# A one-core two-layer attention and mixture kernel: the same steps issued in another order, from a new time table

## What is computed

```python
# cut from the reference
x = x + rotary_attention(conditioned_attention(x, mask, cond))      # 16 heads, causal rotary; inner one 16 heads of 8, rms norm, modulation
x = x + mixture_0(quaternion_filter(x, cond))                       # 8 experts of 128->512->128, the best 2 by a softmax over them
x = x + level_attention(mixture_1(x, cond))                         # 8 experts of 128->256->256->128; decay and level weights, layer norm
x = x + quantised_ffn(conditioned_attention_1(x, mask, cond))       # 128->512, 3-tap conv along the sequence, silu, ->128
```

## Time and profile before

| | us |
|---|---|
| median of 3 runs | 630.21 |
| lowest, highest | 629.35, 632.31 |
| the profiled execution, its own time | 623.68 |
| its span | 621.9 |
| busy in the span: PE, weight loads, VectorE, ScalarE, GpSimd | 473.9, 375.1, 303.5, 246.2, 171.4 |
| mean granted TensorE clock | 0.884 of 2.4 GHz |

### The profile page before, as it was taken

One profiled execution on the slowest core, in us unless ns is written; L12 is line 12 of the kernel. 1 busy time (PEld: TensorE's weight loads), 2 busy tenths in 40 slices (PEclk: granted clock), 3 DMA queues, 4 the chain that ended last, 5 costly groups with the idle time before them and its releaser, 6 DMA issues.

```text
span 621.9 us, 11762 instructions
## 1 busy us (share of the span) xinstructions
PE 473.9 (76%) x4233; PEld 375.1 (60%) x4233; DVE 303.5 (49%) x771; ACT 246.2 (40%) x683; POOL 171.4 (28%) x210
## 2 busy tenths in 40 slices
PE   4897989768989946587776978669998734778875
PEld 4685877557869924466665866544665624566432
DVE  3779655643334427511122247774554003776653
ACT  3545644314575541123332463232554422343311
POOL 5054343172220233550004003455100022232200
PEclk9999989975999977769998998876999985897888
DMA  7977540010444530137786663101263710000000
GB/s 246 325 203 148 160 135 2 2 43 18 132 130 124 154 90 22 47 94 201 185 214 198 171 185 93 27 9 42 61 172 90 182 50 18 2 3 0 1 9 9
DMA packets 50631, 62.13 MB, mean 100 GB/s; under 512 B 6704, under 2 KB 39664, under 8 KB 50320
## 3 DMA queue, kind: packets, MB, share of 16 engines
q1 hardware_dynamic: 48048, 56.88, 33.1%
q0 software_dynamic: 2048, 4.20, 2.3%
q10 hardware_dynamic: 480, 0.32, 0.2%
HBM read 52.86 MB, written 16.94 MB: 112 GB/s over the span
## 4 chain that ended last, share of the span: by engine, by line
PE 55%; DVE 18%; issue 10%; ACT 10%; POOL 3%; another core or an unknown queue 2%; DMA 2%; ACTq 0%; POOLq 0%; DVEq 0%
PE PS L852 6%; PE PS L842 6%; PE PS L826 4%; PE PS L1407 4%; PE PS L1439 4%; PE PS L1834 3%; PE PS L1224 2%; PE PS L1238 2%; PE PS L1421 2%; DVE arena L1735 2%; PE PS L838 2%; PE PS L1213 2%; ACT rot_sm L1494 2%; ACT hid L920 2%
## 5 line engine op out<-in xcount | busy, mean ns | idle before, releaser
L766 POOL DMA_INDIRECT picked<-slots_y,place_u x32 | 31.1, 971 | 109.4 <-DMA slots_y<-slot_y 100.9
L852 PE MATMUL PS<-expert_w,hid 128*128 128x128 f32 x360 | 54.0, 287 | 7.6 <-ACT hid L920 2.7
L852 PEld LDWEIGHTS PS<-expert_w,hid 128*128 128x128 f32 x360 | 46.4, 196 | 14.4 <-issue 10.0
L1072 DVE TENSOR_SCALAR hid<-PS,expert_w 128x128 f32<-128x128 f32 x60 | 18.3, 347 | 75.3 <-PE PS L842 42.2
L842 PE MATMUL PS<-hid,expert_w 128*128 128x128 f32 x240 | 35.7, 296 | 12.5 <-ACT hid L920 9.9
L920 ACT ACTIVATE hid<-PS,expert_w 128x128 f32<-128x128 f32 x120 | 37.4, 366 | 16.7 <-PE PS L826 10.6
L842 PEld LDWEIGHTS PS<-hid,expert_w 128*128 128x128 f32 x240 | 31.3, 204 | 17.0 <-issue 15.8
L826 PE MATMUL PS<-slot_xT,expert_w 128*128 128x128 f32 x240 | 40.0, 293 | 1.9 <-ACT slot_xT L910 1.9
L1439 PE MATMUL PS<-rot_W,rot_yT 128*128 128x128 f32 x256 | 34.3, 298 | 3.7 <-ACT rot_yT L1509 3.7
L1439 PEld LDWEIGHTS PS<-rot_W,rot_yT 128*128 128x128 f32 x256 | 32.8, 211 | 6.9 <-ACT rot_yT L1509 5.7
L826 PEld LDWEIGHTS PS<-slot_xT,expert_w 128*128 128x128 f32 x240 | 33.6, 202 | 4.8 <-ACT slot_xT L910 2.7
(11 more groups left out here) (277 smaller groups left out, 1058.1 us busy)
## 6 DMA issues: line engine op xcount, KB each, us to landing
expert_w<-packed SPq DMA_DIRECT2D x60, 514.0 KB
slot_x<-slots_x SPq DMA_DIRECT2D x60, 64.0 KB
slots_y<-slot_y SPq DMA_DIRECT2D x60, 64.0 KB
...
```

The lines of the kernel that those rows point to most:

```text
L766: nc.gpsimd.indirect_dma_start(picked[:, j, n, :], None, ys[half], bass.IndirectOffsetOnAxis(place_u[job % 2][:, j, n:n + 1], 0)).then_inc ...
L852: mm = nc.tensor.matmul(full(bank_of(MO_, i), 2 * P, 3 * P), hid[:, i % 2, c, :], W[i % WB][:, lo + E * (c - first):lo + E * (c - first) + ...
```

## The change

`TIMES` gets new numbers, nearly all of them. No step is added, removed or changed, and nothing outside the dictionary is touched. Comparing the two sorted orders gives the number of places at which another step stands than before: PE 403 of 526, ScalarE 353 of 457, VectorE 191 of 266, GpSimd 78 of 139, SyncE 64 of 188.

The places that the prediction speaks of:

- `f_taps_of_all` 0 to 3 on PE: before, all four ahead of `m_count` 0; after, all behind it, spread up to the middle of job 0's slots.
- `r_scores` 4 on PE: before, behind `m_biases` 0 and two places ahead of `m_transpose_slots` 0; after, right behind `m_count` 0. The projections of tile 4 come ahead of `m_count` 0.
- `r_times_x` and `r_output` of tiles 6 and 7: before, behind `m_slots_out` 14 (places 201 to 209 of PE, where `m_slots_out` 14 is 200); after, at places 167 to 184, ahead of it (place 208). `r_scores` 6 and 7 move from 197 and 199 to 150 and 170.
- `m_choose` 2 on VectorE: after, right behind `m_choose` 1 and ahead of `m_places` 1. The eight `m_scatter` of jobs 1 and 2 are contiguous on GpSimd, without another step between.
- In job 1, five times `m_hidden_a` of a slot stands ahead of the next slot's `m_transpose_slots` instead of behind it.
- `m_gates` 0 moves from place 331 to 309 of PE, `l_output` 0 from 348 (behind `m_slots_out` 44, which was 344) to 337 (ahead of it, now 349).
- GpSimd after job 2: before `l_inverse_deviation` 0, gathers 8, 9, `c1_spread_keys` 0, `c1_spread_values` 0, gathers 10, 11; after `l_inverse_deviation` 0, `c1_spread_values` 0, `c1_spread_keys` 0, gathers 8 to 11.
- VectorE there, before: combine 8, norm 1, conditioned softmax 0, combine 9, weights of scores 3, `c1_turn` 0, two norm steps, combines 10 and 11, a norm step, `m_squares` 1. After: level weights 2, conditioned softmax 0, norm 1, `c1_turn` 0, combines 8 and 9, weights of scores 2, level weights 3, a norm step, combines 10 and 11, `m_squares` 1.
- PE ahead of `m_transpose_slots` 45: before, eleven steps of `c1_`, `f_` and `m_biases` 3 from `c1_scores` 1 on; after, six of these stand ahead and five behind it.
- At the end, `f_bias` and `f_hidden` of tiles 4 and 5 come ahead of tile 7's `c1_transpose_x` and `c1_scores`.

The diff, cut to the entries of these steps:

```diff
--- before.py
+++ after.py
@@ -116,200 +116,203 @@
...
-    "m_gather": (210.3, 212.5, 214.8, 217, 303, 305.3, 307.5, 309.7, 351.7, 353.9, 358.5, 360.7, 460.4, 462.7, 464.9, 467.2),
-    "m_scatter": (113.9, 116.2, 118.4, 120.6, 233.4, 235.6, 237.8, 240, 245.8, 248.1, 250.3, 252.5, 377.9, 380.1, 382.3, 384.5),
-    "c1_spread_keys": (356.2, 372.2, 387.9, 401.7, 498.3, 501.8, 518.8, 523),
-    "l_inverse_deviation": (350.6, 363, 366.1, 371.2, 491.2, 494.5, 509.6, 513.7),
-    "f_taps_of_all": (86.8, 89.9, 97.9, 106.4),
-    "r_scores": (38.9, 43.9, 70.6, 79, 126, 156.7, 197.5, 202.1),
-    "r_times_x": (55.2, 75.1, 85.8, 92.4, 141.2, 167.7, 210.4, 226.9),
-    "r_output": (67, 82.3, 93.4, 101.4, 144.5, 171, 214.5, 231.1),
-    "m_gates": (335, 475.1),
-    "m_transpose_slots": (129.8, 132.7, 139.1, 140.2, 150.8, 153.5, 154.5, 164.1, 166.6, 168.6, 178.8, 179.8, 185, 188.9, 192.6, 248.4, 249.2, 253.8,
-        254.4, 256.9, 262.7, 265.5, 268.3, 271.9, 274.4, 277.5, 281.1, 284, 286.8, 290.6, 293.4, 296.2, 298.4, 301.1, 303.8, 306.5, 309.3, 313.8,
-        317.2, 324.6, 325.9, 330.6, 333.2, 334, 336.5, 392.9, 395, 397.8, 401.4, 408.1, 409.9, 416.9, 423.8, 430.3, 432.5, 438.1, 440.9, 442.2,
-        445.9, 451.1),
-    "m_choose": (108.3, 227, 239.4, 371.1),
-    "m_combine": (215.6, 217.9, 220.1, 222.5, 308.9, 310.6, 314.1, 317.9, 357, 361.1, 366, 366.7, 465.8, 468, 470.3, 472.5),
-    "c1_turn": (362.2, 383.7, 398.2, 411.2, 503.6, 509.8, 524.6, 532.6),
-    "f_hidden": (384.6, 401.5, 419.6, 427.3, 522.7, 532.7, 544.2, 549.3),
...
+    "m_gather": (225.46, 227.7, 229.94, 232.18, 318.23, 320.47, 322.71, 324.95, 368.2, 370.44, 372.68, 374.92, 476.68, 478.92, 481.16, 483.4),
+    "m_scatter": (120.14, 122.36, 124.58, 127.85, 248.68, 250.88, 253.08, 255.28, 257.48, 259.7, 261.92, 264.14, 392.64, 394.84, 397.04, 399.24),
+    "c1_spread_keys": (366.64, 403.75, 408.26, 442.07, 515.3, 519.99, 538.08, 550.22),
+    "l_inverse_deviation": (355.47, 377.16, 385.21, 401.44, 508.15, 511.48, 528.42, 532.28),
+    "f_taps_of_all": (120.13, 134.76, 161.99, 168.23),
+    "r_scores": (43.83, 50.39, 74.36, 83.1, 117.71, 144.49, 166.38, 183.89),
+    "r_times_x": (71.04, 79.78, 90.46, 94.45, 141.04, 163.07, 180.57, 194.58),
+    "r_output": (76.2, 86.9, 97.85, 106.3, 146.79, 169.09, 186.64, 197.97),
+    "m_gates": (335.04, 491.45),
+    "m_transpose_slots": (136.52, 137.74, 141.97, 151.84, 161.85, 163.99, 175.01, 179.95, 190.66, 192.87, 202.56, 205.43, 207.36, 210.1, 212.6,
+        265.2, 265.47, 270.72, 270.86, 274.05, 279.71, 282.15, 284.19, 288.47, 290.51, 293.37, 297.65, 299.69, 302.55, 306.83, 308.87, 311.73,
+        314.01, 316.91, 319.82, 322.73, 326.45, 329.74, 332.46, 336.7, 343.25, 345.26, 346.53, 350.03, 354.56, 407.56, 410.85, 413.77, 417.59,
+        421.63, 425.47, 428.94, 432.43, 436.74, 444.91, 446.51, 452.99, 457.17, 460.24, 466.81),
+    "m_choose": (113.74, 240.76, 243.67, 385.55),
+    "m_combine": (230.74, 232.98, 235.22, 237.46, 323.5, 326.44, 329.12, 331.81, 375.58, 376.28, 380.87, 381.58, 481.96, 484.2, 486.44, 488.68),
+    "c1_turn": (373.23, 415.55, 417.87, 448.76, 522.84, 528.31, 546.77, 556.33),
+    "f_hidden": (401.91, 432.56, 439.97, 462.61, 537.53, 542.63, 567.72, 575.42),
...
```

More of the change, by code:

```diff
@@ L118 @@
 TIMES = {
[L119 to L131, removed]
@@ new lines @@
+    "l_inverse_deviation": (355.47, 377.16, 385.21, 401.44, 508.15, 511.48, 528.42, 532.28),
[5 rows of a table added]
+    "p_modulations": (11.87,),
+    "c0_scores": (12.4, 14.69, 38.3, 42.86, 65.29, 91.38, 115.47, 143.34),
+    "p_turn_modulations": (17.52,),
+    "r_turn_weights": (16.6, 18.8),
+    "r_fold_weights": (20.79, 29.53, 41.95, 45.67),
[3 rows of a table added]
+    "p_turn_rotation": (31.37,),
[3 rows of a table added]
+    "p_rotations_pe": (36.3,),
+    "r_project_3": (35.28, 41.06, 60.49, 66.25, 112.68, 135.63, 153.27, 178.57),
+    "p_rotated_router": (41.03,),
@@ new lines @@
+    "p_copy_modulations": (18.63,),
+    "r_copy_turned": (17.99, 19.97),
+    "r_copy_folded": (22.76, 30.63, 43.23, 48.84),
[4 rows of a table added]
+    "p_copy_rotation": (31.67,),
+    "r_copy_passed_2": (36.07, 40.33, 64.13, 69.57, 105.6, 134.28, 161.69, 177.6),
+    "p_copy_rotations": (36.96,),
+    "r_copy_passed_3": (37.52, 42.61, 65.35, 70.18, 114.11, 136.71, 162.31, 179.81),
+    "p_copy_router": (41.25,),
+    "r_take_scores": (45.86, 57.05, 76.39, 86.24, 119.74, 146.52, 168.42, 185.92),
+    "r_exponentials": (51.47, 64.75, 82.96, 91.38, 133.24, 153.65, 173.55, 191.51),
@@ new lines @@
+    "f_copy_yqT": (408.63, 445.69, 453.37, 469.52, 546.63, 556.68, 578.83, 582.53),
+    "p_router": (9.28,),
+    "p_gated_condition": (11.08,),
+    "p_spread_condition": (8,),
+    "p_casts": (9.85,),
+    "p_mask_bias": (9.03,),
+    "p_norms": (11.77,),
+    "p_gains": (12.72,),
+    "c0_softmax_in": (14.73, 17.27, 39.44, 46.82, 71.65, 94.35, 120.03, 144.48),
+    "c0_turn": (19.32, 21.62, 43.73, 51.25, 76.3, 97.1, 123.75, 149.58),
+    "p_rotations": (25.29,),
+    "f_magnitudes": (23.92,),
[5 rows of a table added]
@@ L313 @@
+    "f_quantise_x": (393.62, 426.73, 431, 457.62, 532.81, 536.56, 559.8, 565.89),
+    "f_gate": (405.34, 436, 443.43, 466.06, 540.98, 546.09, 573.77, 578.88),
+    "f_quantise_y": (406.03, 436.68, 446.69, 466.74, 541.67, 549.46, 574.46, 579.56),
+    "f_finish": (412.16, 451.08, 456.42, 470.8, 549.09, 558.65, 581.63, 583.8),
 }
```

198 lines of the change are left out of this document (82 added, 116 removed), and 111 rows, old and new, of the table TIMES.

## The result

| | before | changed |
|---|---|---|
| median of 20 runs each, us | 629.39 | 630.50 |
| lowest, highest | 615.04, 640.60 | 625.91, 638.26 |
| profiled execution, its span | 623.68, 621.9 | 633.15, 631.4 |
| mean granted clock | 0.884 | 0.869 |

The medians of all 20 are only 0.2% apart; the ratio of the runs within 1.5% of the fastest of their kernel (5 of the 20 before, 17 of the 20 changed) is 1.016 (95% interval 1.0112 to 1.0208). Single executions of one kernel scatter by some 2% around their median here, so the comparison was made twice more with both kernels beside each other: 1.0137 (1.0067 to 1.0207) and 1.0223 (1.016 to 1.0285). The kernel before against itself gave 0.996 (0.9907 to 1.0013) and 1.0018 (0.9969 to 1.0067). The forecast was 615 and "faster"; it was wrong in sign, and the loss rests on the three ratios together.

The account below looks back on a forecast made before the run. PE was taken to bound the slots, and the gather, combine, choose, scatter chain the waits between jobs. The terms -1 -3 +5 -1.5 -1 -14 +1 -1 gave -15.5: 608.2 us profiled, 615 on the median, range 600 to 629.

Parts of the forecast that it names:

- +5: Job 0's slots (145 to 223): rotary tails and taps come in, projections leave; 5 us longer, from 0 to +12.
- 223 to 267: Wait after job 0: tails leave, the routing and scatter chain stays; -1.5 us, from -4 to +2.
- The main term, -14: Wait after slot 44 (377 to 436): shorter chain to job 3's first transpose, 2.9 + 6 + 1 + 4; from -16 to -7.
- The "6" between gather and squares: Wait after slot 44: gathers together and most DVE work after them save 6 of up to 7.8 us.
- The "4" behind the scatter: Last scatter to job 3's first transpose: six instead of eleven PE steps in front, 4 us less.
- "Level-attention work enters beside 26.6 us idle": Job 1 and 2 slots (267 to 377): about 5 us of tile 0 work enters; -1 us, from -8 to +4.
- rival "slower": Rotary steps of tiles 4 to 7 stall PE's in-order queue within slots, 20.6 us more: 635.3 us; chance 0.11.
- 124 to 145: -3: Before job 0's first transpose: tile 4's 64 score matmuls, 3.84 us, move ahead of the first scatter; -3 us.
- rival "no change": Moved work finds no gap in job 0's slots (+12), wait after slot 44 gives only 7: 628.7 us; chance 0.11.
- rival "more gain": Waits close also in the head, jobs 1 to 3 and the tail, another 12 us: 603 us; chance 0.20.
- 436 to 505: +1: Job 3's slots: leftover c1 and FFN steps, about 4.6 us in 10.1 idle; +1 us, from 0 to +5.
- 505 to 622: -1: End after the last gathers: order nearly the same, two small swaps; -1 us, from -3 to +2.

Follow-up runs that it names:

- set 3: Kernel before and changed kernel each run a third time without edits, beside each other on one chip, with two edited kernels: ratios 1.0018 and 1.0223 for the unedited two.
- chain_first: Changed kernel with job 3's combines, squares, choice of experts and dependent steps moved ahead of tile 0's conditioned softmax; ratio 1.0187 to the kernel before.
- old_tails_new: Kernel before with only the steps from first count to mid-wait after job 0 in the new order, conv taps left in the head; ratio 1.0296.
- after_warm: Changed kernel plus 192 unused constant matmuls ahead of PE's waits between slots 14 and 15; ratio 1.0217 to the kernel before.
- sets 1 and 4: Set 1: both kernels repeated (0.996, 1.0137), two reordered. Set 4: job 2's or both stretches undone in the changed kernel, filler matmuls in both kernels; 1.0004 to some 1.032.
- sets 2 and 3: Set 2: kernel before with head, tails or end alone reordered (1.0132, 1.0296, 1.0022), and an extended chain-first kernel (1.0302). Set 3: both kernels repeated (1.0018, 1.0223), two edited.
- old_head_new: Kernel before with only the steps up to the first count in the new order among themselves; ratio 1.0132.

## Why the prediction was wrong, by its steps

| stretch of the kernel before | forecast | first profiles | set 3 |
|---|---|---|---|
| 0 to 124 | -1 | +3.2 | -3.1 |
| 124 to 145 | -3 | -0.2 | +0.2 |
| 145 to 223 | +5 | +6.8 | +8.0 |
| 223 to 267 | -1.5 | -1.9 | -1.0 |
| 267 to 377 | -1 | +1.1 | +4.0 |
| 377 to 436 | -14 | -6.6 | -7.5 |
| 436 to 505 | +1 | +4.1 | +1.3 |
| 505 to 622 | -1 | +2.9 | +2.1 |
| sum | -15.5 | +9.4 | +4.0 |

Each column is one profiled execution against another: the columns are not the ratios, and in set 3 the head (0 to 124) of the kernel before was itself some 8 us longer than in its first profile.

**The main term, -14, held in one of its four parts.** Its parts, as end of slot 44 to gather, gather to squares, squares to end of last scatter, that to the first transpose: before 7.7, 21.4, 20.4, 9.8; changed 4.8, 21.65, 21.5, 4.65; in set 3 before 7.7, 17.9, 21.1, 5.8 and changed 4.6, 15.9, 19.3, 5.1. The 2.9 of the gather is right to 0.2 in both. The "6" between gather and squares was 0 and 2, the "1" behind it a loss of 1.1 and a gain of 1.8. The prediction read in the diff that softmax, norm and turn of tile 0 stand ahead of combines 8 and 9, and yet wrote "most of that DVE work after them"; `chain_first`, with the combines really ahead, brought the squares 9 us nearer to slot 44, some 3 of them by the order itself. The stretch of 5.29 "with no releaser seen" was counted as belonging to the order and thus as recoverable. The trace puts 3.7 of it to a late update of PE's semaphore (L1679 ends at 394.00, its update is at 397.70): it is gone in the kernel before in set 3, and grew to part of the 10.96 in the changed kernel where such updates occur. The "4" behind the scatter came in the first pair (5.1), but in set 3 the baseline had it already (5.8). So the forecast wait of 45 was measured, 45.3; against 52.8 of the same set, though, and not against 59.5.

**"Level-attention work enters beside 26.6 us idle", -1 for slots 15 to 44, failed.** From slot 29 to slot 44 PE's busy time grew by 5.9 us in set 3 (40.4 to 46.3) and the time by 6.7. The idle was no store to be filled: where rows of the slots were read, it consists of short waits between dependent steps (0.26 to 0.91 us). The same for job 0's slots, where +5 was +7 to +8 for 4 to 5 us more of busy PE; the term there was undersized by 2 to 3. In the end this is the general mistake of the sum: it treats work that leaves a wait as gained where it was, and lets it be absorbed where it goes. In waits it had been nearly free, since POOL, DMA and VectorE set their length: 14 to 17 us less of busy PE after job 0 bought 1.0 to 1.9 us. Of the stretches, job 0's slots show this most directly, since `old_tails_new` re-sorted that part alone: +7.4 us there, a ratio of 1.0296.

**124 to 145: -3 failed** since the 64 scores left and others took their place. In the changed kernel of set 3 the four projections of tile 5 stand there instead (24 matmuls and, behind c0 and tap steps, 8 more), and the first transpose is queued behind them as before behind L1421:

```profile
141.74 5.35 PE L1410 MATMUL PS<-featT,rot_wqk 128*128 128x128 f32 x24
...
149.34 0.27 PE L821 MATMUL PS<-const,slot_x 128*128 128x128 f32 x1
```

**223 to 267 held**, -1.0 to -1.9 for -1.5. So did the argument that its path is not PE's, and the fall of the clock, which cost about 1 us there and, by the one profile of `after_warm`, perhaps 3 in job 1's slots. "No L1430 waiting over 2 us" held as well (0.2 us at most), so the rival "slower" did not come by its head-of-line stalls. Nearest in its terms was the rival "no change", 628.7 (the changed kernel's median was 630.50, but by its ratio of 1.016 it lost more than even the rival "slower", 635.3 or 1.008): it had 12 more in job 0's slots and 7 less in the wait after slot 44, measured were 7 to 8 and 7. It was given 0.11, as the gaps in the slots had been seen to be short and were yet counted as room. In the rival "more gain" the sum is off: its five terms stand against -3.5 of the forecast, not -2, so that three quarters of the difference are 11 and not 12; nothing hangs on it.

**436 to 505: +1** was +4.1 and, in set 3, +1.3. The new order took 71.3 to 72.3 us there in all its profiles, the old one 68.1 or 70.3 to 70.5, so the size of this term depends on which profile of the kernel before is taken.

**505 to 622: -1 failed**, +2 to +3. The new order of the end alone costs next to nothing (113.2, against 112.5 and 110.9). Behind the changed front part the same steps in the same order took 114.6 to 119.4, with 43 to 54 us at the low clock instead of 33 to 43. Why the low stretches are longer there stays open, and so does the head, whose -1 was +3.2 and -3.1: the new one came in at 124.2 to 128.3 where the rest of the new table followed (129.1 in `old_head_new`), the old one at 122.7 to 123.9 in the first profile and sets 1 and 4 and at 128.9 to 133.1 in sets 2 and 3.
